# A wavelet convolution: two more images loaded ahead of the second half, and a shorter hand-over of the first batch's last coefficients

## The chip, the cores and the metric

The kernel runs on one core of one Trainium2 chip. The metric is the device time of one execution in microseconds (us), lower is better. The time of a kernel is the median over its runs.

## The reference

The input `x` has 8 batches of 32 channels, each channel a 512x512 float32 image (1 MB). Each image goes through a four-level wavelet transform. The coarsest level (a low band and three detail bands of 42x42 each, 84x84 together) is mixed over the channels, for each coefficient with a 32x32 matrix of its own; the finer detail bands stay as they are. Then the transform is inverted.

```
yl, yh = _dwt2(x, 4)
yl_out = einsum('bixy,ioxy->boxy', yl, w_yl)
yh_out = yh[:-1] + [einsum('bicxy,iocxy->bocxy', yh[-1], w_yh)]
return _idwt2(yl_out, yh_out)
```

Since all steps are linear and the finer bands come back unchanged, the output is `x` plus the inverse transform of (mixed minus unmixed coarse coefficients). That is how the kernel computes it.

## The kernel before

It works in three phases, with an order written out by hand for each engine and semaphores between them.

Phase 1 (from the start to about 662 us) reads all 256 images once, on SP's queue, and reduces each to 84x84 coefficients.

The mixing (to about 739 us) goes through 32 pieces (`PIECES`), of the 84x84 coefficients of all batches. SP loads the weights of a piece into a ring of four places in `work` (`w_sb`, `load_w`). ScalarE and VectorE spread the coefficients of a piece into a diagonal operand (`diag`, two of them, `build_high` and `build_low`), TensorE multiplies (`mix`, L474 and L479), ScalarE copies the sums from PSUM into `mix_sb` (`copy_mixed`, L611). Along with it, the coefficients of the first batch to be written (batch 7) are brought into the form that phase 2 needs, in six steps v = 0 to 5: ScalarE copies a step from `mix_sb` to `first_stage` (`copy_first`, L618), TensorE turns it (`first_coefs`, L488), ScalarE copies it to `delta` (`copy_delta`, L627). The last step, v = 5 (`FULL`), needs the sums of the last piece, number 31.

Phase 2 (to the end) reads the images again, adds the correction and writes them, batch 7 first. The image of one channel takes: a copy of its coefficients to `pick` (`pick_image`, L667, ScalarE), a matrix product (`spread_stage`, L518), a copy (`copy_spread`, L673), four products (`out_stage`, L528), two additions on VectorE (`add`, L759), in place in the buffer of the image, and the store (`store`, L344, on SP's queue). One turn is eight images (`SLOTS`), for the eight buffers of `x_sb`; there are 32 turns. The eight images of turn 0 are still in `x_sb` from phase 1. GpSimd (POOL) refills a buffer when its store has landed (`refill`, L280), in the order of its own instructions: what stands first in it holds up all behind it.

Of the images of turn 1, number 8 to 15 of phase 2, the first six (`EARLY` = 6) are loaded ahead into `work`, which is no longer needed by then (`load_early`, L320 and L323): three during phase 1 and the mixing, and three behind the last pieces. They are stored from there (L351). Images 14 and 15 come by a refill of buffers 6 and 7 of `x_sb`. So the refills are: images 16 to 21 for buffers 0 to 5 and 14 and 15 for buffers 6 and 7 behind the stores of turn 0; then images 22 and 23 for buffers 6 and 7, behind the stores of images 14 and 15; then turn by turn.

The other things that lie in `work`: `w_sb` at 6784 to 13952 (in elements of a partition), `diag` at 13952 to 17536, and in phase 2 `delta` for two batches in turn, 2688 elements each from 4096 and from 13000, and `stage` (the next batch's coefficients, L658) from 15688. The early images lie at 0, 2048, 19184, 6784, 8832 and 10880, 2048 elements each.

Of the kernel before, what the change touches and what calls it, by code (L numbers as in the profile page):

```python
# [22 lines left out]
BATCH, CHANNELS, SIZE = 8, 32, 512  # L23
# [29 lines left out]
TURNED = {1: 0, 2: 1, 4: 2, 5: 3, 7: 4, 8: 5}  # L53
IDLE = ROUNDS + 1 - STEPS

EARLY = 6

WARM = 9

# [83 lines left out]
def last_piece(s):  # L143
    return len(LEFT) + PARTS * s - 1


def wavelet_mix_kernel(nc, x, w_full, w_left, consts, out):
# [3 lines left out]
    with ExitStack() as ctx:  # L151
# [41 lines left out]

        early = [0, IMAGE, AT_EARLY] + [AT_W + IMAGE * e for e in range(EARLY - 3)]
        early = [work[:, e:e + IMAGE].rearrange("p (r w) -> p r w", r=ROW_RUN) for e in early]
        APART = -(-(AT_W + IMAGE * (EARLY - 3) - 2 * IMAGE) // ROWS)
        at = 2 * IMAGE + (APART + CHANNELS) * ROWS
        delta = work[:, 2 * IMAGE:at].rearrange("p (a r) -> p a r", r=ROWS)
        assert at + STEPS * Q * ROWS <= AT_EARLY
# [69 lines left out]
        @block.gpsimd  # L269
        def _(pool):  # L270
            nc.gpsimd.memset(work[:, IMAGE:AT_W], 0.0).then_inc(pass1_cleared, 1)
            nc.gpsimd.memset(mix_sb[:, 0], 0.0).then_inc(cleared, 1)
            nc.gpsimd.memset(pick[:], 0.0).then_inc(cleared, 1)
            nc.gpsimd.memset(spread[:], 0.0).then_inc(cleared, 1)


            def refill(c, t, first):

                pool.wait_ge(x_stored[c], 16 * (t - (c < EARLY)))
                pool.dma_start(x_sb[:, c], x_rows[first + c]).then_inc(x_reloaded[c], 16)  # L280

            for c in range(SLOTS):
                if c < EARLY:
                    refill(c, 2, IMAGES - 3 * SLOTS)
                else:
                    refill(c, 1, IMAGES - 2 * SLOTS)
            for c in range(EARLY, SLOTS):
                refill(c, 2, IMAGES - 3 * SLOTS)
            with pool.Fori(3, TURNS) as t:
                first = t * -SLOTS + (IMAGES - SLOTS)  # L290
                for c in range(SLOTS):
                    refill(c, t, first)

        @block.sync
        def _(sp):
            sp.dma_start(const[:, 0:SW], consts[:, 0:SW]).then_inc(const_loaded, 16)


            for c in range(SLOTS):
                sp.dma_start(x_sb[:, c], x_rows[c]).then_inc(x_loaded[c], 16)  # L300
                if c == GROUP - 1:
                    sp.dma_start(const[:, SW:CONSTS], consts[:, SW:CONSTS]).then_inc(more_loaded, 16)
            with sp.Fori(1, TURNS) as t:
                for c in range(SLOTS):
                    if c % GROUP == 0:
                        sp.wait_ge(h_done[c // GROUP], t)
                    sp.dma_start(x_sb[:, c], x_rows[SLOTS * t + c]).then_inc(x_loaded[c], 16)  # L307


            def load_w(k):  # L310
                c = k % RING
                if k < len(LEFT):
                    u = LEFT[k]
                    sp.dma_start(w_sb[:, c, 0:u * 4 * CHANNELS], w_left[k, :, 0:u * 4 * CHANNELS]).then_inc(w_loaded[c], 16)
                else:
                    sp.dma_start(w_sb[:, c], w_full[k - len(LEFT)]).then_inc(w_loaded[c], 16)

            def piece_mixed(k):

                sp.wait_ge(mixed[k % 2], k // 2 + 1)  # L320

            def load_early(e):
                sp.dma_start(early[e], x_rows[IMAGES - 2 * SLOTS + e]).then_inc(early_loaded[e], 16)  # L323

            for k in range(RING):
                load_w(k)
            load_early(2)
            sp.wait_ge(t_done, TURNS * SLOTS)
            load_early(0)
            sp.wait_ge(c_done, TURNS * HALVES + 1)  # L330
            load_early(1)
            for k in range(RING, PIECES):
                piece_mixed(k - RING)
                load_w(k)
            for e in range(3, EARLY):
                piece_mixed(PIECES - RING + e - 3)
                piece_mixed(PIECES - RING + e - 2)
                load_early(e)

            def store(c, t, first):
                sp.wait_ge(added[1], SLOTS * t + c + 2)
                sp.dma_start(out_rows[first + c], x_sb[:, c]).then_inc(x_stored[c], 16)  # L344

            for c in range(SLOTS):
                store(c, 0, IMAGES - SLOTS)
            for c in range(SLOTS):
                if c < EARLY:
                    sp.wait_ge(added[1], SLOTS + c + 2)  # L350
                    sp.dma_start(out_rows[IMAGES - 2 * SLOTS + c], early[c]).then_inc(early_stored, 16)  # L351
                else:
                    store(c, 1, IMAGES - 2 * SLOTS)
            with sp.Fori(2, TURNS) as t:
                first = t * -SLOTS + (IMAGES - SLOTS)
                for c in range(SLOTS):
                    store(c, t, first)
            sp.wait_ge(early_stored, 16 * EARLY)
            for c in range(SLOTS):
                sp.wait_ge(x_stored[c], 16 * (TURNS - (c < EARLY)))  # L360

        @block.tensor
        def _(pe):
# [149 lines left out]
            def spread_stage(c, t):  # L513

                p, n = c % 2, SLOTS // 2 * t + c // 2
                pe.wait_ge(picked[p], n + 1)
                pe.wait_ge(s_copied[p], n + 1)
                nc.tensor.matmul(ps[0:ROWS, p], pick[:, p], const[:, SW:SW + SIZE],  # L518
                                 start=True, stop=True).then_inc(s_done[p], 1)

            def out_stage(c, t):

                p, n = c % 2, SLOTS * t + c
                pe.wait_ge(s_copied[p], SLOTS // 2 * t + c // 2 + 2)
                for half in range(2):
                    pe.wait_ge(added[half], n + 1)
                    for k in (2 * half, 2 * half + 1):
                        last = nc.tensor.matmul(ps[:, 2 + k], const[:, SH + P * k:SH + P * k + P], spread[:, p],  # L528
                                                start=True, stop=True)
                    last.then_inc(o_done[half], 1)  # L530
# [10 lines left out]
                        coefs_stage(2 * (c - 1) + 1, batch)  # L541

            pe.wait_ge(cleared, 4)
            spread_stage(0, 0)
            with pe.Fori(0, BATCH - 1) as k:
                with pe.Fori(0, TURNS_BATCH - 1) as r:
                    turn2(TURNS_BATCH * k + r)
# [6 lines left out]
        def _(act):  # L554
# [59 lines left out]
            def copy_first(v, i):  # L614
# [3 lines left out]
                nc.scalar.copy(first_stage[:].rearrange("p (q r) -> p q r", q=Q), mix_sb[:, v, :, :, BATCH - 1],  # L618
                               ).then_inc(first_staged, 1)

            def copy_delta(v, k, done):
                n, h = lines(v), first_row(v)
                bank = (6 + v % 2) if done is None else 6
                act.wait_ge(d_done, STEPS * k + v + 1 + IDLE if done is None else done)
                to = delta[0:ROWS, bass.ds(APART * (k & 1), CHANNELS), h:h + Q * n]
                of = ps[0:ROWS, bank].rearrange("p (q l o) -> p o l q", q=Q, l=4)[:, :, 0:n]
                nc.scalar.copy(to.rearrange("p o (l q) -> p o l q", q=Q), of).then_inc(d_copied, 1)  # L627
# [9 lines left out]
            for k in range(PIECES):  # L637
                if k % RING == 0 and k // RING not in TURNED:
                    act.sem_inc(first_staged, 1)
                if k + 2 < PIECES:  # L640
                    build_high(k + 2)
                copy_mixed(k)
                i, j = divmod(k, RING)
                if j == 2:
                    if i in TURNED:
                        copy_delta(TURNED[i], 0, i + 1)
                    else:
                        act.wait_ge(d_done, i + 1)
                        act.sem_inc(d_copied, 1)
                for at, v in TURNED.items():  # L650
                    if k == last_piece(v):
                        copy_first(v, at)


# [19 lines left out]

            def turn2(t, last=False, batch=None):
                for c in range(SLOTS):
                    if batch is not None and 2 <= c <= 4:
                        copy_delta(2 * (c - 2), batch, None)
                        copy_delta(2 * (c - 2) + 1, batch, None)
# [13 lines left out]

            copy_delta(FULL, 0, ROUNDS + 1)
            act.wait_ge(d_copied, STEPS + IDLE + 1)
            pick_image(0, 0)
            pick_image(1, 0)
            copy_spread(0, 0)
            with act.Fori(0, BATCH - 1) as k:
# [8 lines left out]
        def _(dve):  # L708
# [53 lines left out]
            for c in range(SLOTS):  # L762
                add(c, 0, x_sb[:, c])
            for c in range(SLOTS):
                if c < EARLY:
                    dve.wait_ge(early_loaded[c], 16)
                    add(c, 1, early[c])
                else:
                    dve.wait_ge(x_reloaded[c], 16)
                    add(c, 1, x_sb[:, c])  # L770
            with dve.Fori(2, TURNS) as t:
                for c in range(SLOTS):
                    dve.wait_ge(x_reloaded[c], 16 * (t - (c < EARLY)))
                    add(c, t, x_sb[:, c])


# [25 lines left out]
```

## Time and profile before

| | |
|---|---|
| median of 3 runs | 1996.33 us (1993.37 to 1996.72) |
| the profiled execution | 2000.08 us, its span 1998.4 us |
| mean granted clock of TensorE | 0.994 |
| busy: PE, DVE, ACT, POOL | 94%, 41%, 24%, 7% |
| moved by DMA | 827.04 MB, 414 GB/s over the span |
| read, written | 558.29 MB, 268.44 MB |

The engines in the rows are PE (TensorE matmul), PEld (its weight load), DVE (VectorE), ACT (ScalarE), POOL (GpSimd), SP (SyncE, which only issues transfers here). Times of the trace are us from the start of the span. The span lies 1.7 us below the profiled execution's time. A matrix product in float32 appears as two MATMUL records.

### The profile page before, as it was taken

Reading aid. Unit: us, or ns where it says so; the run is one execution under the profiler, and the core shown is the slowest. Engines: PE = TensorE matmul, PEld = TensorE weight load, DVE = VectorE, ACT = ScalarE, POOL = GpSimd, SP = SyncE. Lnnn points to the kernel's source line nnn. Section 1 sums busy time; section 2 is a strip of 40 time slices with the busy share of each in tenths; the row PEclk is TensorE's granted clock in tenths of the full one; section 3 lists DMA queues with packets and bytes.
Section 4 is the critical chain, followed back from the end, with each engine's and each line's share of the span. In section 5 each row is a group of like instructions: output and inputs, shape, how many; then the busy total and the mean of one; then the engine's idle time right before and its main releaser. Section 6 shows DMA issues by size and latency. Waiting matters only on the chain.

```text
span 1998.4 us, 44611 instructions
## 1 busy us (share of the span) xinstructions
PE 1873.2 (94%) x17701; PEld 939.1 (47%) x17701; DVE 810.9 (41%) x931; ACT 483.7 (24%) x1055; POOL 135.7 (7%) x250
## 2 busy tenths in 40 slices
PE   8999999999999899999999999999999999999996
PEld 5666666666666554444343343343343343333332
DVE  2222222222222345555444444444444444444443
ACT  2233232332332551221221121121121121122110
POOL 1000000000000000011111111111111111111110
PEclk9999999999999999999999999999999999999999
DMA  9999999999999899999999999999999999999997
GB/s 369 415 415 421 418 422 422 422 422 422 422 422 421 313 375 387 367 427 427 427 427 427 427 427 427 427 427 427 427 427 427 427 427 426 416 427 419 417 425 336
DMA packets 114355, 827.04 MB, mean 414 GB/s; under 512 B 12704, under 2 KB 12704, under 8 KB 17056
## 3 DMA queue, kind: packets, MB, share of 16 engines
q1 hardware_dynamic: 79488, 573.01, 68.9%
q0 software_dynamic: 34848, 253.77, 30.4%
q8 instruction: 13, 0.21, 0.0%
q14 instruction: 6, 0.05, 0.0%
HBM read 558.29 MB, written 268.44 MB: 414 GB/s over the span
## 4 chain that ended last, share of the span: by engine, by line
DMA 61%; PE 30%; issue 4%; DVE 2%; SPq 1%; ACT 0%; DVEq 0%; POOLq 0%; ACTq 0%
DMA out<-x_sb 33%; DMA x_sb<-x 28%; PE ps L388 10%; PE ps L528 7%; PE ps L401 5%; DVE x_sb L759 2%; PE ps L518 2%; PE ps L479 2%; PE ps L474 2%; SPq L307 1%; PE ps L412 1%; PE ps L420 1%; PE ps L434 1%; ACT mix_sb L581 0%; PE ps L488 0%
## 5 line engine op out<-in xcount | busy, mean ns | idle before, releaser
L528 PE MATMUL ps<-spread,const 128*128 128x512 f32 x2048 | 940.1, 602 | 75.4 <-DVE x_sb L759 75.4
L759 DVE TENSOR_TENSOR x_sb<-ps,x_sb 128x1024 f32<-128x1024 f32 x500 | 592.9, 1221 | 632.2 <-DMA x_sb<-x 546.9
L528 PEld LDWEIGHTS ps<-spread,const 128*128 128x128 f32 x2048 | 373.5, 190 | 640.0 <-issue 406.8
L673 ACT COPY spread<-ps 84x512 f32<-84x512 f32 x256 | 148.8, 581 | 923.9 <-PE ps L518 922.4
L388 PE MATMUL ps<-x_sb,const 32*32 32x512 f32 x8192 | 286.7, 597 | 20.6 <-DMA x_sb<-x 17.3
L401 PEld LDWEIGHTS ps<-const,work 128*128 128x128 f32 x2048 | 246.6, 193 | 52.6 <-ACT work L565 38.1
L518 PE MATMUL ps<-const,pick 128*84 128x512 f32 x512 | 261.3, 592 | 1.0 <-issue 1.0
L401 PE MATMUL ps<-const,work 128*128 128x84 f32 x2048 | 255.6, 277 | 0.0
L280 POOL DMA_DIRECT2D x_sb<-x x242 | 128.1, 529 | 1837.0 <-DMA out<-x_sb 1837.0
L565 ACT COPY work<-ps 128x512 f32<-128x512 f32 x256 | 131.4, 600 | 416.6 <-PE ps L388 416.6
L388 PEld LDWEIGHTS ps<-x_sb,const 32*32 32x32 f32 x8192 | 138.1, 103 | 119.7 <-issue 79.7
L718 DVE COPY work<-ps 128x336 f32<-128x336 f32 x256 | 130.0, 508 | 153.3 <-PE ps L401 153.3
L724 DVE COPY work<-ps 128x336 f32<-128x336 f32 x65 | 33.0, 508 | 338.0 <-PE ps L412 338.0
L518 PEld LDWEIGHTS ps<-const,pick 128*84 128x84 f32 x512 | 77.3, 153 | 121.9 <-issue 121.9
L667 ACT COPY pick<-work 84x84 f32 (+1 forms) x256 | 66.7, 261 | 10.7 <-issue 10.7
L744 DVE COPY work<-mix_sb 32x448 f32<-32x448 f32 (+1 forms) x96 | 36.4, 379 | 39.5 <-PE ps L479 36.3
L412 PE MATMUL ps<-work,const 128*32 128x336 f32 x520 | 50.8, 463 | 0.6 <-DVE work L718 0.6
L420 PE MATMUL ps<-work,const 128*84 128x336 f32 x130 | 48.2, 452 | 0.6 <-DVE work L724 0.6
L479 PEld LDWEIGHTS ps<-work 128*32 128x32 f32 x3584 | 37.3, 110 | 21.6 <-DMA work<-w_full 10.7
L479 PE MATMUL ps<-work 128*32 128x32 f32 x3584 | 38.1, 199 | 3.3 <-issue 3.3
L627 ACT COPY work<-ps 84x512 f32 (+3 forms) x48 | 24.0, 529 | 55.8 <-PE ps L508 54.4
L571 ACT COPY work<-ps 84x336 f32 (+1 forms) x65 | 28.2, 434 | 37.6 <-PE ps L420 37.6
(30 smaller groups left out, 301.4 us busy)
## 6 DMA issues: line engine op xcount, KB each, us to landing
x_sb<-x SPq DMA_DIRECT2D x256, 1024.0 KB, 10.1
out<-x_sb SPq DMA_DIRECT2D x250, 1024.0 KB, 24.6
x_sb<-x POOLq DMA_DIRECT2D x242, 1024.0 KB, 11.7
work<-w_full SPq DMA_DIRECT2D x30, 896.0 KB, 7.3
work<-x SPq DMA_DIRECT2D x6, 1024.0 KB, 5.6
out<-work SPq DMA_DIRECT2D x6, 1024.0 KB, 9.7
work<-w_left SPq DMA_DIRECT2D x1, 896.0 KB, 15.0
const<-consts SPq DMA_DIRECT2D x1, 592.0 KB, 12.2
```

The costliest lines, as they stand in the source:

```text
L280: pool.dma_start(x_sb[:, c], x_rows[first + c]).then_inc(x_reloaded[c], 16)
L388: last = nc.tensor.matmul(ps[to:to + TILE, m], const[part, A3H + TILE * r:A3H + TILE * r + TILE], x_sb[part, GROUP * a + m, r], start=r == ...
L401: last = nc.tensor.matmul(ps[:, 4 + m % 2, ROWS * k:ROWS * k + ROWS], along_h[:, m, P * k:P * k + P], const[:, A4 + ROWS * m:A4 + ROWS * ( ...
L412: last = nc.tensor.matmul(ps[TILE * k:TILE * k + TILE, 6, 0:GROUP * ROWS], const[:, at:at + TILE], turned[:, k].rearrange("p m r -> p (m r ...
L420: nc.tensor.matmul(ps[0:ROWS, 7, 0:GROUP * ROWS], const[:, A4:A4 + ROWS], third, start=True, stop=True).then_inc(c_done, 1)
L479: last = nc.tensor.matmul(ps[32 * l:32 * l + 32, j, QB * u:QB * u + QB], w[:, u, l], diag[:, a, l, u], start=False, stop=u == U - 1)
L518: nc.tensor.matmul(ps[0:ROWS, p], pick[:, p], const[:, SW:SW + SIZE], start=True, stop=True).then_inc(s_done[p], 1)
L528: last = nc.tensor.matmul(ps[:, 2 + k], const[:, SH + P * k:SH + P * k + P], spread[:, p], start=True, stop=True)
L565: nc.scalar.copy(along_h[:, m], ps[:, m]).then_inc(h_copied, 1)
L673: nc.scalar.copy(spread[0:ROWS, p], ps[0:ROWS, p]).then_inc(s_copied[p], 1)
L718: nc.vector.tensor_copy(turned[:, :, m], ps[:, 4 + m % 2, 0:SEGS * ROWS].rearrange("p (k r) -> p k r", k=SEGS),).then_inc(t_copied, 1)
L759: nc.vector.tensor_tensor(part, ps[:, 2 + 2 * half:4 + 2 * half], part, ALU.add).then_inc(added[half], 1)
```

## The change

The program loads eight early images. `EARLY` is 8; the two new ones lie at 12928 and 14976, over the last place of the weight ring and both diagonal operands, so that they are loaded, like image 5 of the early ones, behind the matmuls of piece 31. All of turn 1 is then computed in `work` and stored from there, and POOL's first eight refills are for turn 2. The second `delta` and `stage` move down and overlap early images 5 to 7, so ScalarE waits for all early stores at the start of turn 3, ahead of the first copies of the next batch.

The last step of the first batch is split. The 70 of 84 columns that come from pieces 26 to 30 are copied from `mix_sb` behind `copy_mixed(30)` (`copy_last_first`), and the 14 columns of piece 31 are copied from PSUM straight to `first_stage` ahead of `copy_mixed(31)` (`copy_last_piece`). The first image's product reads its coefficients from `delta` and not from `pick` (`first_spread`).

```diff
-EARLY = 6
+EARLY = 8
...
-        APART = -(-(AT_W + IMAGE * (EARLY - 3) - 2 * IMAGE) // ROWS)
+        APART = -(-(AT_W + IMAGE * 2 - 2 * IMAGE) // ROWS)
...
             def refill(c, t, first):
-                pool.wait_ge(x_stored[c], 16 * (t - (c < EARLY)))
+                pool.wait_ge(x_stored[c], 16 * (t - 1))
                 pool.dma_start(x_sb[:, c], x_rows[first + c]).then_inc(x_reloaded[c], 16)
             for c in range(SLOTS):
-                if c < EARLY:
-                    refill(c, 2, IMAGES - 3 * SLOTS)
-                else:
-                    refill(c, 1, IMAGES - 2 * SLOTS)
-            for c in range(EARLY, SLOTS):
                 refill(c, 2, IMAGES - 3 * SLOTS)
...
             for e in range(3, EARLY):
-                piece_mixed(PIECES - RING + e - 3)
-                piece_mixed(PIECES - RING + e - 2)
+                piece_mixed(min(PIECES - RING + e, PIECES + 1) - 3)
+                piece_mixed(min(PIECES - RING + e, PIECES + 1) - 2)
                 load_early(e)
...
             for c in range(SLOTS):
-                if c < EARLY:
-                    sp.wait_ge(added[1], SLOTS + c + 2)
-                    sp.dma_start(out_rows[IMAGES - 2 * SLOTS + c], early[c]).then_inc(early_stored, 16)
-                else:
-                    store(c, 1, IMAGES - 2 * SLOTS)
+                sp.wait_ge(added[1], SLOTS + c + 2)
+                sp.dma_start(out_rows[IMAGES - 2 * SLOTS + c], early[c]).then_inc(early_stored, 16)
...
+            def first_spread():
+                pe.wait_ge(d_copied, STEPS + IDLE + 1)
+                nc.tensor.matmul(ps[0:ROWS, 0], delta[0:ROWS, CHANNELS - SLOTS], const[0:ROWS, SW:SW + SIZE],
+                                 start=True, stop=True).then_inc(s_done[0], 1)
...
-            spread_stage(0, 0)
+            first_spread()
...
+            def copy_last_first():
+                n = U * (PARTS - 1)
+                act.wait_ge(mixed_copied, RING + PIECES - 1)
+                act.wait_ge(d_done, ROUNDS)
+                nc.scalar.copy(first_stage[:].rearrange("p (q r) -> p q r", q=Q)[:, :, 0:n],
+                               mix_sb[:, FULL, :, 0:n, BATCH - 1])
+            def copy_last_piece():
+                k, n = PIECES - 1, U * (PARTS - 1)
+                act.wait_ge(mixed[k % 2], k // 2 + 1)
+                (_, of), = sums_of(k)
+                nc.scalar.copy(first_stage[:].rearrange("p (q r) -> p q r", q=Q)[:, :, n:ROWS],
+                               of[:, :, :, BATCH - 1]).then_inc(first_staged, 1)
...
+                if k == PIECES - 1:
+                    copy_last_piece()
                 copy_mixed(k)
+                if k == PIECES - 2:
+                    copy_last_first()
...
-                    if k == last_piece(v):
+                    if k == last_piece(v) and v < FULL:
                         copy_first(v, at)
...
+                    if batch is not None and c == 0:
+                        act.wait_ge(early_stored, 16 * EARLY)
...
-            pick_image(0, 0)
+            act.sem_inc(picked[0], 1)
             pick_image(1, 0)
...
             for c in range(SLOTS):
-                if c < EARLY:
-                    dve.wait_ge(early_loaded[c], 16)
-                    add(c, 1, early[c])
-                else:
-                    dve.wait_ge(x_reloaded[c], 16)
-                    add(c, 1, x_sb[:, c])
+                dve.wait_ge(early_loaded[c], 16)
+                add(c, 1, early[c])
```

## Rows read from the trace of the kernel before

**Rows 1.** The page, the span in 40 slices of 50 us: share of DMA, rate.
```profile
DMA  9999999999999899999999999999999999999997
GB/s 369 415 415 421 418 422 422 422 422 422 422 422 421 313 375 387 367 427 427 427 427 427 427 427 427 427 427 427 427 427 427 427 427 426 416 427 419 417 425 336
```

**Rows 2.** The page, the chain that ended last, by engine.
```profile
DMA 61%; PE 30%; issue 4%; DVE 2%; SPq 1%; ACT 0%; DVEq 0%; POOLq 0%; ACTq 0%
```

**Rows 3.** Chain in order of time: start, us, what; one image and the last transfers.
```profile
808.85 3.43 PE ps L528 x8
812.28 0.86 PE ps L518 x2
...
1947.42 24.67 DMA out<-x_sb
...
1972.84 11.67 DMA x_sb<-x
```

**Rows 4.** Stretches: length, busy time of each engine, PEclk, DMA share, GB/s.
```profile
740.00:744.60 4.60, 2.83 (x9) 1.20 (x10) 0.00 (x0) 2.48 (x7) 0.00 (x0) 1.00 0.99 388
744.60:750.50 5.90, 5.90 (x15) 2.57 (x14) 2.45 (x2) 1.45 (x5) 0.00 (x0) 1.00 0.12 47
...
806.00:815.00 9.00, 9.00 (x22) 3.84 (x21) 5.00 (x5) 1.58 (x4) 0.53 (x1) 1.00 0.63 259
```

**Rows 5.** Timeline of SP's queue, 730 to 860 us: start, time from first to last.
```profile
735.03 4.69 SPq L323 DMA_DIRECT2D work<-x  x3
749.20 30.38 SPq L344 DMA_DIRECT2D out<-x_sb  x8
783.53 21.79 SPq L351 DMA_DIRECT2D out<-work  x6
809.28 47.69 SPq L344 DMA_DIRECT2D out<-x_sb  x12
```

**Rows 6.** Timeline of POOL: the 1st, 8th, 9th, 16th, 42nd, 201st, 209th and last refill.
```profile
753.76 0.66 POOL L280 DMA_DIRECT2D x_sb<-x  x1 [745.49 <-DMA out<-x_sb]
...
789.51 0.54 POOL L280 DMA_DIRECT2D x_sb<-x  x1 [4.53 <-DMA out<-x_sb]
813.54 0.53 POOL L280 DMA_DIRECT2D x_sb<-x  x1 [23.49 <-DMA out<-x_sb]
...
850.75 0.53 POOL L280 DMA_DIRECT2D x_sb<-x  x1 [4.34 <-DMA out<-x_sb]
...
978.42 0.53 POOL L280 DMA_DIRECT2D x_sb<-x  x1 [4.38 <-DMA out<-x_sb]
...
1768.87 0.53 POOL L280 DMA_DIRECT2D x_sb<-x  x1 [4.42 <-DMA out<-x_sb]
...
1808.97 0.53 POOL L280 DMA_DIRECT2D x_sb<-x  x1 [4.58 <-DMA out<-x_sb]
...
1972.84 0.54 POOL L280 DMA_DIRECT2D x_sb<-x  x1 [4.45 <-DMA out<-x_sb]
```

**Rows 7.** Timeline at the end of the mixing, ACT and PE, and one copy in turn 2.
```profile
737.81 0.58 ACT L627 COPY work<-ps 84x512 f32<-84x512 f32 x1
...
739.35 0.53 ACT L611 COPY mix_sb<-ps 128x448 f32<-128x448 f32 x1 [0.96 <-PE ps L479]
739.91 0.79 ACT L618 COPY const<-mix_sb 128x336 f32<-128x336 f32 x1
...
740.76 0.64 PE L488 MATMUL ps<-const 128*84 128x128 f32 x4 [1.45 <-ACT const L618]
741.43 0.58 ACT L627 COPY work<-ps 84x512 f32<-84x512 f32 x1 [0.73 <-PE ps L488]
742.04 0.42 ACT L667 COPY pick<-work 84x84 f32<-84x84 f32 x2
...
742.40 1.92 PE L518 MATMUL ps<-const,pick 128*84 128x512 f32 x4 [1.01 <-issue]
...
843.30 0.58 ACT L673 COPY spread<-ps 84x512 f32<-84x512 f32 x1 [3.55 <-PE ps L518]
```

More of the change, by code:

```diff
@@ L359, in _ @@
             for c in range(SLOTS):
-                sp.wait_ge(x_stored[c], 16 * (TURNS - (c < EARLY)))
+                sp.wait_ge(x_stored[c], 16 * (TURNS - 1))
         @block.tensor
@@ L764, in _ @@
             for c in range(SLOTS):
-                if c < EARLY:
-                    dve.wait_ge(early_loaded[c], 16)
-                    add(c, 1, early[c])
-                else:
-                    dve.wait_ge(x_reloaded[c], 16)
-                    add(c, 1, x_sb[:, c])
+                dve.wait_ge(early_loaded[c], 16)
+                add(c, 1, early[c])
             with dve.Fori(2, TURNS) as t:
                 for c in range(SLOTS):
-                    dve.wait_ge(x_reloaded[c], 16 * (t - (c < EARLY)))
+                    dve.wait_ge(x_reloaded[c], 16 * (t - 1))
                     add(c, t, x_sb[:, c])
```

## The prediction

> **What bounds the kernel now.** I read the slices of the page first: the DMA engines are busy in nearly all of them, at up to 427 GB/s, and the low slices (313, 375, 387, 367 GB/s) all lie between 650 and 850 us, where the phases change [rows 1]. The chain says the same: 61% of the span is DMA and 30% PE [rows 2]. So what counts is where the DMA engines stand idle, and the view to go to is the one of stretches. Loads end at about 744.6 us; in the 5.9 us behind that the DMA share is 0.12, since the mixing is over and no image has been finished; and from 806 to 815 it is 0.63 [rows 4].
>
> The second gap shows in the queues. SP stores one image after the other: 8 from `x_sb` from 749.20 on, 6 from `work`, and the next at 809.28, which is 14 images on, so (809.28 - 749.20) / 14 = 4.29 us for an image [rows 5]. That is PE's own time, 0.86 for the spread product and 3.43 for the four others [rows 3]. This stretch goes at PE's pace. POOL issues its first 8 refills from 753.76 to 789.51 us, and then nothing for 23.5 us: its ninth needs the store of image 14 and comes at 813.54 [rows 6]. Meanwhile the DMA engines have one store of 1.05 MB per 4.29 us, 2.46 us of work at 427 GB/s, a share of 0.57, as seen.
>
> From the ninth refill on it is otherwise. From refill 42 at 978.42 to refill 242 at 1972.84 there are 200, at 4.97 us each [rows 6]: a load and a store, 2.10 MB, at 422 GB/s. For a while PE still runs ahead on images loaded early, but that uses up a lead and doesn't move the end. At the end the chain is store, refill, addition, store [rows 3]. So I cut the time in two at the ninth refill: ahead of it the pace is PE's, behind it the DMA engines'.
>
> **The hand-over, part by part.** In the profile the last piece's sums are ready at 739.35. Then follow in one line the copy to `mix_sb` (0.53), the copy to `first_stage` (0.79), the turning on PE (from 740.76, 0.64), the copy to `delta` (from 741.43, 0.58), the pick (from 742.04, two in 0.42), and the first product at 742.40: 3.05 us [rows 7]. With the change the copy of 14 columns comes first. No row shows it: 128 partitions x 56 elements. Its ends are 0.21 us (half of the 0.42 for two copies of 84 columns) and 0.53 (a copy of 448 from PSUM) [rows 7]; I take 0.26, near the small one. Then 739.35 + 0.26 + 0.06 (from copy to PE) + 0.67 (PE start to the next copy's start) + 0.58 + 0.10 = 741.0. The copy to `mix_sb` moves behind it and ends at about 740.1, under PE's turning. Gain 1.4 us, with the large copy 1.1.
>
> The 70-column copy is new on ACT behind `copy_mixed(30)`, ahead of the copy of step 4 to `delta`. ACT has 739.35 - 738.39 = 0.96 us free there [rows 7]; it takes about 0.79 x 280 / 336 = 0.66, at most 0.79. It is covered with 0.2 to 0.3 us to spare; if copies in a row that depend on each other add a little, the gain falls to 0.9. I keep 0.9 to 1.4. Its waits are on work that ended before.
>
> **The two early images.** Their loads go to SP's queue behind piece 31, right behind the load of image 5 of the early ones [rows 5]. They take 2 x 2.46 = 4.9 us, from 744.6 to 749.5, nearly all of the first gap [rows 4]. The first store, issued 1.4 us earlier at 747.8, stands behind them in the queue and lands at about 752.9, not 753.8; that costs nothing, as refills 1 to 8 (now images 16 to 23) are far ahead of their use. Nothing waits for the two images until 744 + 14 x 4.29 = 804 us.
>
> What it moves is the cut. POOL's ninth refill is now image 24, which needs the store of image 16. PE's pace holds until there: that store is issued at 749.20 - 1.4 + 16 x 4.29 = 816.5 and lands after 813.54 - 809.28 = 4.26 us, at 820.7 [rows 5, 6]. That is 7.2 us later than before, as the idle gap at 806 grows by two more images. Behind it, there are 240 refills in all and not 242, so the last comes 231 and not 233 periods later: 2 x 4.97 = 9.9 us less. The lead of the loads on PE at the cut is the same as before (refill 9 with images 15 to 17 in work there), so what follows should repeat itself two images later.
>
> **The added wait.** ScalarE waits at turn 3 for all early stores. Behind it are queued its picks and spread copies, and PE behind them. It gets there at about 843.9 - 1.4 us, by its last copy of turn 2 at 843.30 [rows 7]; the last early store, of image 15, is issued at 812.1 and lands some 4 to 6 us later. More than 20 us of slack: nothing. The other edits (smaller semaphore counts, one product from `delta`) cost nothing that a row could show; the PE clock is at 1.00 in both stretches of the hand-over [rows 4].
>
> **Sum.** -1.4 (hand-over) + 2 x 4.29 - 2 x 4.97 = -2.76 us. In other words: two more images go at PE's pace and not at DMA's, which returns 0.68 us each, not the 4.9 us that their loads take. The profiled execution of 2000.08 us would become 1997.3. It stands 3.75 us above the median; taken off the median, 1996.33 - 2.76 = 1993.6 us, a gain of 0.14%. About 0.2%, 4.0 us, is what a measurement of this kernel can tell from no change, so the likeliest verdict is no difference.
>
> **A rule against the row.** The 4.97 us per image is 422 GB/s with one core at work [rows 6]. The Trainium skill (DMA: Bandwidth & Descriptors, section Where 436 GB/s comes from) says that for transfers between HBM and SBUF the HBM side binds, at about 358 GB/s. By that an image would cost 5.86 us and the sum would be -1.4 - 2 x (5.86 - 4.29) = -4.5 us, an estimate from that page; the trace disagrees with it in every slice of phase 2, and the sum goes by the trace.
>
> **The rivals.**
> 1. A larger gain, by the restart. Behind the ninth refill the transfers find their order anew: refills 9 to 16 take 850.75 - 813.54 = 37.2 us for 7 periods, 2.4 us more than 7 x 4.97; refills 1 to 8 took 35.75, 1.0 more [rows 6]. If the restart is better when it begins in order at buffer 0, up to 2.4 us come on top: 1991.2. If the bytes alone counted, as a DMA share of 61% in the chain suggests [rows 2], the two loads would return all of their 4.9 us and with the hand-over 6.3: 1990.0. Against that speaks the gap at 806, which grows. Together 0.27.
> 2. A memory-bound pace as in the restart (5.32 us per image there): -1.4 - 2 x (5.32 - 4.29) = -3.5 us, 1992.9, still within 0.2%. The later rows hold it for 200 refills at 4.97. 0.02.
> 3. Slower, by the pace of the loop of 8 buffers. The steady pace isn't given by the bytes alone: turns differ, and the one from 1768.87 to 1808.97 has 5.01 per refill [rows 6]. The new start may lock loads and stores into another pattern. Over 231 periods 0.012 us more in each (4.984) eats the gain, and 0.029 (5.001) makes it slower by 0.2%. At 5.01 throughout it would be 231 x 0.04 = 9.3 us, with the gain 2002.8; with half of that 1998.2. One turn of 25 is like that, so 0.07.
> 4. It doesn't do what it says: the 70-column copy isn't covered, and the restart loses 1 to 2 us more than before, since image 16's store has to share with image 17's. 1995 to 1996.5; 0.06.
>
> **How the numbers follow.** Forecast 0.58, rivals 0.27, 0.02, 0.07, 0.06. Rival 1 is faster by over 0.2% in most cases, and the forecast's own spread (0.9 to 1.4 for the hand-over, about 1.5 for the restart) passes the bound now and then: faster 0.27, within 0.2% 0.66, slower 0.07. The range reaches from rival 1's far half to rival 4's upper end: 1990.2 to 1996.8 leaves out about half of rival 1's lowest case and rival 3.
>
> **What would show it.** Right: the first L518 at about 741.0; the last early loads landing at 749 to 750 with no gap in DMA ahead of the first store; no refill of POOL from about 789 to 821, with a DMA share near 0.57 from 806 to 820; the ninth refill at 820.7 and the last, number 240, near 1970; 4.97 us between late refills. Wrong: another steady pace, a ninth refill well before 820, ScalarE waiting at turn 3, or a restart that takes more or less than 37 us for its first 7 periods.

## The result and the profile after

The changed kernel takes 1993.61 us in the median of 12 runs (1991.11 to 1995.31), the kernel before in the same series 1997.30 us (12 runs, 1993.37 to 2001.31). The ratio is 0.9977, with a 95% interval of 0.9968 to 0.9986: 4.6 us less by the ratio, 3.7 by the medians. Forecast were 2.76 us less. Two more measurements on other chips, told below, gave 0.9985 and 0.9983.

The profiled execution of the changed kernel has a span of 1991.8 us, 6.6 us below that of before. I take it apart along the path that the prediction laid out.

The timeline at the end of the mixing, ACT and PE; it answers to [rows 7]:

```profile
735.08 0.72 ACT L625 COPY const<-mix_sb 128x280 f32<-128x280 f32 x1
...
736.49 0.21 ACT L633 COPY const<-ps 128x56 f32<-128x56 f32 x1 [0.20 <-PE ps L472]
736.59 0.54 ACT L610 COPY mix_sb<-ps 128x448 f32<-128x448 f32 x1
...
736.75 0.64 PE L481 MATMUL ps<-const 128*84 128x128 f32 x4 [0.30 <-ACT const L633]
737.42 0.58 ACT L642 COPY work<-ps 84x512 f32<-84x512 f32 x1 [0.29 <-PE ps L481]
...
738.14 1.06 PE L517 MATMUL ps<-const,work 84*84 84x512 f32 x2 [0.76 <-ACT work L642]
```

The last sums are ready at 736.49 and the first product of phase 2 starts at 738.14: 1.65 us, where it was 3.05. The copy of 14 columns (L633) has 0.21 us, that of 70 columns (L625) 0.72, and the latter is over before it could be in the way: ACT waits 0.20 us for PE ahead of L633. But the sums themselves are ready 2.86 us earlier than in the profile of before. The first load behind the mixing goes out the same 2.86 us earlier, and what the change puts ahead of the last sums is only the copy of 70 columns, which is work more and not less; so this part doesn't come from the change.

SP's queue, then POOL's refills: the 1st, 8th, 9th, 16th and last. They answer to [rows 5] and [rows 6].

```profile
732.17 5.64 SPq L319 DMA_DIRECT2D work<-x  x5
744.93 30.38 SPq L340 DMA_DIRECT2D out<-x_sb  x8
779.27 30.37 SPq L346 DMA_DIRECT2D out<-work  x8
813.77 44.09 SPq L340 DMA_DIRECT2D out<-x_sb  x11
```

```profile
751.38 0.66 POOL L281 DMA_DIRECT2D x_sb<-x  x1 [743.11 <-DMA out<-x_sb]
...
786.74 0.54 POOL L281 DMA_DIRECT2D x_sb<-x  x1 [3.95 <-DMA out<-x_sb]
818.44 0.53 POOL L281 DMA_DIRECT2D x_sb<-x  x1 [31.16 <-DMA out<-x_sb]
...
856.13 0.53 POOL L281 DMA_DIRECT2D x_sb<-x  x1 [4.41 <-DMA out<-x_sb]
...
1966.00 0.53 POOL L281 DMA_DIRECT2D x_sb<-x  x1 [4.43 <-DMA out<-x_sb]
```

Five early loads go out from 732.17, the first store follows 12.76 us behind the first of them (14.17 before). From the first store to the ninth refill it is 73.51 us (64.34 before), from there to the last refill 1147.56 (1159.30 before), from there to the end 25.8 (25.6 before). So the 6.6 us are: 2.9 ahead of the sums, 1.4 in the hand-over, -9.2 up to the ninth refill, 11.7 behind it, -0.2 at the end. Of the 11.7, two periods of 4.97 are 9.9; the other 1.8 are 231 periods that were each 0.008 us shorter.

The stretches of [rows 4] in the changed kernel:

```profile
740.00:744.60 4.60, 4.60 (x12) 2.07 (x12) 2.14 (x2) 0.90 (x3) 0.00 (x0) 1.00 1.00 399
744.60:750.50 5.90, 5.90 (x15) 2.54 (x14) 2.76 (x3) 1.48 (x4) 0.00 (x0) 1.00 0.87 368
806.00:815.00 9.00, 9.00 (x22) 3.84 (x21) 4.97 (x5) 1.49 (x5) 0.00 (x0) 1.00 0.58 239
...
804.00:820.00 16.00, 16.00 (x39) 6.93 (x38) 9.12 (x8) 3.07 (x8) 0.53 (x1) 1.00 0.57 235
```

The first gap is gone (a DMA share of 0.87 where it was 0.12), and the second is longer: 16 us at a share of 0.57. Since all marks lie 2.86 us earlier here, the stretch that stands as far behind the last sums as 744.6 to 750.5 did before is 741.7 to 747.6: there the share is 1.00 at 418 GB/s. That is the exchange: the two loads fill the first gap, and the second takes most of the gain back.

### The profile page after: what moved, and what is told of

It reads as the page before. It is cut to its first block, busy times and chain, and to the rows that moved or that the text cites. A ratio compares the mean times of both kernels' runs of the same rounds, so it can differ in the third digit from the quotient of the medians.

```text
span 1991.8 us, 44554 instructions
## 1 busy us (share of the span) xinstructions
PE 1870.6 (94%) x17701; PEld 936.8 (47%) x17701; DVE 810.4 (41%) x931; ACT 483.7 (24%) x1055; POOL 134.7 (7%) x248
## 4 chain that ended last, share of the span: by engine, by line
DMA 61%; PE 30%; issue 4%; DVE 2%; SPq 1%; ACT 0%; DVEq 0%; POOLq 0%; ACTq 0%
DMA out<-x_sb 32%; DMA x_sb<-x 29%; PE ps L381 10%; PE ps L527 7%; PE ps L394 5%; DVE x_sb L780 2%; PE ps L511 2%; PE ps L472 2%; PE ps L467 1%; SPq L303 1%; PE ps L405 1%; PE ps L413 1%; PE ps L427 1%; ACT mix_sb L580 0%; PE ps L481 0%
## 5 line engine op out<-in xcount | busy, mean ns | idle before, releaser
L527 PE MATMUL ps<-spread,const 128*128 128x512 f32 x2048 | 940.2, 602 | 73.5 <-DVE x_sb L780 73.5
L765 DVE COPY work<-mix_sb 32x448 f32<-32x448 f32 (+1 forms) x96 | 36.4, 379 | 37.5 <-PE ps L472 32.4
L472 PE MATMUL ps<-work 128*32 128x32 f32 x3584 | 37.5, 198 | 3.5 <-issue 3.5
```

The lines of the kernel that those rows point to most:

```text
L472: last = nc.tensor.matmul(ps[32 * l:32 * l + 32, j, QB * u:QB * u + QB], w[:, u, l], diag[:, a, l, u], start=False, stop=u == U - 1)
```

## The experiments

The theory: up to the ninth refill the time goes at PE's pace, behind it at the DMA engines'; the change gives 1.4 us by the hand-over and about 1.4 by two images that change sides. Its rivals: the bytes alone count; the restart behind the ninth refill gives more; the gain is chance.

**The hand-over alone.** On the kernel before:

```diff
-            spread_stage(0, 0)
+            first_spread()
...
+                if k == PIECES - 1:
+                    copy_last_piece()
                 copy_mixed(k)
+                if k == PIECES - 2:
+                    copy_last_first()
```

> The kernel before with the hand-over alone (the 14 columns straight from PSUM, the first product from delta); six early images. Two-pace theory: the first product comes 1.4 us earlier behind the last piece's sums, PE's pace carries that to the ninth refill, and the end comes 1.4 us earlier (ratio to before 0.9993). Rival, bytes alone: the loads and stores that are left are the same, so 0. Rival, a chance difference of the profiled executions ahead of the mixing: a change of 1 to 3 us that is not there in this one.

Measured: 1995.22 us (12 runs), ratio 0.9990 with 0.9980 to 1.0000. Its first product (737.66) comes as soon behind the last sums as in the changed kernel, and the first store 12.9 us behind the first of the early loads from `x`. From the first store to the ninth refill it has 64.32 us, as before. The place of the gain in the trace is as the theory has it; its size, 2.0 us by the ratio, can't be told from 1.4, and hardly from 0.

**The early images alone.** The changed kernel with the hand-over of before:

```diff
-EARLY = 6
+EARLY = 8
...
             spread_stage(0, 0)
```

> The changed kernel with the hand-over of before; eight early images. Two-pace theory: two images at 4.29 us and not at 4.97, 1.4 us less (ratio to before 0.9993); the ninth refill stands 8.6 us later behind the first store than before, at 64.3 + 8.6 = 72.9 us. Rival, bytes alone: both loads come back whole, 4.9 us less (0.9975), and the measured 3.7 to 4.6 us of the whole change would be nearly all from here. Rival, restart: 1.4 us and up to 2.4 more.

Measured: 1995.93 us, ratio 0.9989 with 0.9979 to 0.9999. From the first store to the ninth refill 73.50 us, the same as in the changed kernel. The 4.9 us (0.9975) of the bytes alone lie outside the interval, if only just. The traces say it more clearly. From the first store to the end the five profiles of kernels with eight early images and nothing else changed behind the first store (the changed kernel three times, this run, and the later start below) have 1245.3 to 1247.7 us, in the mean 1246.9; the three with six (the kernel before twice, and the hand-over alone) have 1246.6 to 1249.2, in the mean 1247.5. That is 0.6 us less and not 4.9: the rival that the loads come back whole is out. That each half holds a part of the gain is what the traces show; by the totals alone it isn't shown, since the changed kernel's ratios lie inside the intervals of both halves.

**The changed kernel again.** No edit.

> The changed kernel once more, on the same chip as its two halves. Two-pace theory: the sum of the halves, 2.8 us less than before (0.9986). Measured earlier: 0.9977 with an interval of 0.9968 to 0.9986; if it comes near 0.9977 again, 1.9 us are not explained by the sum. The granted clock at 662 us and the pace of the late refills are to be compared in this profile: before had 0.50 there and 4.97 us, the changed kernel 1.00 and 4.96.

Measured: 1994.03 us, ratio 0.9985 with 0.9974 to 0.9996. From the first store to the ninth refill 73.52 us; from the ninth to the 16th refill 37.1 us (37.7 in its first profile, 37.2 before). The restart is the same, so rival 1's first reason is out too.

**The gap filled.** Places 0 to 4 of the early images are free for all of phase 2 once they are stored. Five images of turn 3 are loaded there, right behind the first eight refills:

```diff
+            for c in range(AGAIN):
+                pool.wait_ge(early_stored[c], 16)
+                pool.dma_start(early[c], x_rows[IMAGES - 4 * SLOTS + c]).then_inc(early_again[c], 16)
+            for c in range(AGAIN):
+                refill(c, 4, IMAGES - 5 * SLOTS)
             for c in range(AGAIN, SLOTS):
                 refill(c, 3, IMAGES - 4 * SLOTS)
```

`AGAIN` is 5, `early_stored` is a semaphore for each place, and SP and VectorE take these five images from `work`.

> The changed kernel with five images of turn 3 loaded into the places in work that are free from then on, behind the stores of the early images there. Two-pace theory: the idle time of DMA between the eighth and the ninth refill (804 to 820 us at a share of 0.57, 6.9 us idle) is filled with 5 loads of 2.46 us, and the restart behind it falls away (up to 2.4 us): 5 to 9 us less than the changed kernel, ratio to before 0.993 to 0.9955. Rival, the gap is idle time that costs nothing because the steady loop of eight buffers sets the end: no gain over the changed kernel, 0.9977.

Measured: 1987.95 us (5 runs), ratio 0.9949 with 0.9936 to 0.9962. On another chip, next to the changed kernel:

> The kernel with the gap filled, on the same chip as the changed kernel. Two-pace theory: as measured, 6 to 7 us less than the changed kernel, ratio to before 0.9949 again.

Measured: 1986.54 us (6 runs), ratio 0.9938 with 0.9924 to 0.9952; the changed kernel there 1994.38. It is 6 to 8 us faster than the changed kernel and 10 to 12 faster than the one before. POOL's refills in this second profile, the 8th to the 10th and the 13th and 14th, and its stretches:

```profile
785.27 0.54 POOL L288 DMA_DIRECT2D x_sb<-x  x1 [3.46 <-DMA out<-x_sb]
790.11 0.53 POOL L291 DMA_DIRECT2D work<-x  x1 [4.31 <-DMA out<-work]
795.08 0.53 POOL L291 DMA_DIRECT2D work<-x  x1 [4.43 <-DMA out<-work]
...
809.74 0.53 POOL L291 DMA_DIRECT2D work<-x  x1 [4.32 <-DMA out<-work]
825.57 0.53 POOL L284 DMA_DIRECT2D x_sb<-x  x1 [15.30 <-DMA out<-x_sb]
```

```profile
804.00:820.00 16.00, 16.00 (x38) 6.81 (x37) 9.05 (x8) 3.07 (x8) 1.06 (x2) 1.00 1.01 427
820.00:840.00 20.00, 20.00 (x48) 8.53 (x47) 11.75 (x10) 3.76 (x10) 2.12 (x4) 1.00 1.01 426
...
860.00:900.00 40.00, 40.00 (x101) 17.50 (x100) 22.60 (x19) 8.00 (x21) 2.65 (x5) 1.00 0.95 375
```

The refills run on through 809.74, and from 804 to 820 the DMA engines are at 1.01 and 427 GB/s. The 6.9 us that stood idle there in the changed kernel are about what the end gains. POOL still pauses 15.3 us, but loads are queued up then. From 860 to 900 a small gap is left (0.95). That the idle time of DMA in this place is worth its length at the end is shown, within the some 3 us that the intervals leave, and that it costs nothing is out.

**A later start.** Ten more products of 128x512 behind the last turning, on the changed kernel:

```diff
             first_coefs(ROUNDS)
+            for n in range(10):
+                nc.tensor.matmul(ps[:, 7], const[:, 0:P], const[:, 0:SIZE], start=True, stop=True)
```

> The changed kernel with ten more 128x512 products on TensorE behind the last turning of the hand-over (10 x 0.86 = 8.6 us, of which 0.75 fall into PE's wait for the copy to delta), so the first product of phase 2 comes 7.9 us later behind the last sums. Two-pace theory: a late start of phase 2 costs its whole length at the end, +7.9 us over the changed kernel, and 1.4 us of hand-over are 1.4 us of the end. Rival, the lead of the loads or the early images cover part of the start: less than +4.

Measured: 2001.27 us (10 runs), ratio 1.0018 with 1.0006 to 1.0031. From the first early load to the first store 20.39 us, 7.63 more than in the changed kernel. Against the changed kernel's three ratios (mean 0.9982) the time is 0.0036 up, 7.2 us. Behind the first store nothing gave way: 73.50 us to the ninth refill and 1247.1 to the end, as in the changed kernel. A late start costs its whole length. That the hand-over's 1.4 us are 1.4 at the end is concluded from this; the totals can't resolve it.

**More work for PE, ahead of the cut and behind it.** One more product of 256 columns in an image, `extra` set in turns 0 and 1, or in three turns of four from turn 4 to 27:

```diff
                     out_stage(c, t)
+                    if extra:
+                        nc.tensor.matmul(ps[:, 7, 0:256], const[:, 0:P], const[:, 0:256], start=True, stop=True)
```

> The changed kernel with one more product of 256 columns on TensorE for each of the 16 images of turns 0 and 1 (0.43 us each by half of 0.86; the spacing of the stores will tell). Two-pace theory: this stretch goes at PE's pace, so the ninth refill comes 16 x 0.43 = 6.9 us later and the end with it. Rival, the whole of phase 2 is bound by DMA: 0.

> The changed kernel with the same added product for each of the 144 images of three turns in four from turn 4 to 27: 62 us of added PE work. Two-pace theory: behind the ninth refill the pace is DMA's, 4.96 against 4.29 + 0.43 = 4.72, so 0 to +1 us. Rival, PE sets the pace in part, or the steady pace of 4.96 depends on how long an image takes between its load and its store (one of three stations of the loop of eight buffers): +144 x a part of 0.43, up to 60 us.

Measured: ahead of the cut 2003.30 us, ratio 1.0021 (1.0007 to 1.0036), which is 7.8 us over the changed kernel's 0.9982. SP's queue and the ninth refill of this kernel:

```profile
746.22 33.40 SPq L340 DMA_DIRECT2D out<-x_sb  x8
784.00 33.40 SPq L346 DMA_DIRECT2D out<-work  x8
821.96 4.60 SPq L340 DMA_DIRECT2D out<-x_sb  x2
```

```profile
826.64 0.53 POOL L281 DMA_DIRECT2D x_sb<-x  x1 [37.36 <-DMA out<-x_sb]
```

The stores come every 4.72 us, and the ninth refill 80.42 us behind the first store, 6.9 later, as expected. Behind the cut: 1996.15 us, ratio 0.9988 (0.9973 to 1.0004), 1.2 us over 0.9982, which lies inside the interval of 3 us to each side, for 62 us of added work. PE's waits for the additions fell from 73.5 us to 22.6: the added work went mostly into time in which PE stood idle. Its refills from the ninth on come every 4.98 us. These two runs show the cut most plainly: 6.9 us of PE work cost 7.8 on one side of it, 62 us cost about nothing on the other.

**Thirteen buffers.** The five places in `work` stay in use to the end, for every second turn:

```diff
+            with pool.Fori(2, TURNS // 2) as j:
+                for c in range(AGAIN):
+                    load_x(c, 2 * j, j)
+                for c in range(AGAIN, SLOTS):
+                    load_x(c, 2 * j - 1, 2 * j - 2)
+                for c in range(AGAIN):
+                    load_e(c, 2 * j + 1, j)
+                for c in range(AGAIN, SLOTS):
+                    load_x(c, 2 * j, 2 * j - 1)
```

> The kernel with the gap filled, and the five places in work kept in use to the end: 13 buffers and not 8, buffers 0 to 4 of x_sb in even turns, the five in work in odd ones. It asks what sets the steady pace. If the loop of eight buffers holds it at 4.95 to 4.97 us for an image (before, refills 9 to 41 went at 4.91 while PE ran ahead): with five more buffers 4.91, so 200 x 0.05 = 8 to 12 us less than the kernel with the gap filled, about 1977 us. Rival, 4.95 is what the DMA engines give for loads and stores in turn, whatever the buffers: no change, 1986 to 1988 us.

> The kernel with thirteen buffers, on the same chip as the one with the gap filled. If the count of buffers sets the steady pace, it is 8 to 12 us faster than that one; if the DMA engines set it, the same within 2 us. Its first profile had 1241.2 us from the first store to the end against 1237.7 with the gap filled, which speaks for the second.

Measured: 1985.24 us (4 runs, 0.9928, 0.9908 to 0.9948) and on the other chip 1986.83 (6 runs, 0.9940, 0.9925 to 0.9956), next to 1986.54 with the gap filled. On one chip the two are 0.3 us apart, and the 8 to 12 us are not there. The totals alone would not settle it, since this kernel has an idle stretch of its own near the end: from 1900 to 1950 us its DMA share is 0.90 and 0.89 in its two profiles, where it is 1.01 with the gap filled. The pace does settle it: from the 60th to the 200th refill one takes 4.97 us in both profiles with thirteen buffers, 4.95 and 4.96 with the gap filled, and the DMA share from 1000 to 1400 us is 1.01 in all of them, so that the lower clock told of below doesn't hide a gain either. So more buffers don't make the steady pace faster.

The 4.91 us that the expectation names held for refills 16 to 42 in the first profile of before (from the ninth on it is 5.00, with the restart). The three profiles of the changed kernel show such a step too, from 4.91 to 4.92 us before it to 4.96 to 4.97 behind it. The second profile of before, told of next, doesn't: there these refills took 4.97 each, and those from the 60th to the 200th 4.95. Why the pace went from 4.91 us to 4.97 near 973 us stays open.

**What two equal kernels differ by.**

> The kernel before, once more, with a second profile. It gives what two equal kernels differ by here: ratio 1.000 and an interval of about 0.001 to each side. In its profile the first store to the ninth refill should be 64.3 us again (PE's pace), while the granted clock at 662 us and the pace of the late refills (4.97 before, 4.95 to 4.97 elsewhere) are free to differ: if they do, they belong to the execution and not to the change.

> The changed kernel a third time. By the parts as the traces measured them (hand-over -1.4, two early images +9.2 - 9.9 = -0.8) -2.2 us, ratio 0.9989; by the prediction's sum 0.9986; by the first two measurements 0.9977 and 0.9985. A third ratio near 0.998 would leave about 1.5 us that no part of the sum holds.

Measured: the kernel before 1996.45 us, ratio 0.9994 (0.9982 to 1.0006); the changed kernel 1994.38, ratio 0.9983 (0.9973 to 0.9994). The second profile of the kernel before has a span of 1994.7 us. Its store of image 14 and its ninth and last refills:

```profile
748.08 30.38 SPq L344 DMA_DIRECT2D out<-x_sb  x8
782.41 21.79 SPq L351 DMA_DIRECT2D out<-work  x6
808.16 47.68 SPq L344 DMA_DIRECT2D out<-x_sb  x12
```

```profile
813.37 0.53 POOL L280 DMA_DIRECT2D x_sb<-x  x1 [22.81 <-DMA out<-x_sb]
...
1970.08 0.54 POOL L280 DMA_DIRECT2D x_sb<-x  x1 [4.39 <-DMA out<-x_sb]
```

From the first store to the ninth refill it has 65.29 us, not the 64.3 expected: the store of image 14 took 5.2 us to land and not 4.3. From there 233 periods take 1156.7 us, 4.964 each, against 4.976 in the first profile. The early loads start at 733.91, not 735.03. So an equal kernel was 3.7 us shorter in its span: 1.1 by its start, 2.6 by the pace and 0.9 behind the last refill, less 0.95 for the landing of that store.

## Why the prediction was right

**The range and the direction held.** Forecast 1993.6 us, measured 1993.61. That the two agree so closely is luck: the forecast was 2.76 us off a median of 1996.33, and with more runs the kernel before lies at 1997.3 to 1998.5 by the series. In the first series the start was 1.0 us too low and the gain 0.9 too small, and the two cancel. What was forecast is the difference: 2.76 us, against 4.6, 3.0 and 3.4 us by the three ratios (0.9977, 0.9985, 0.9983), in the mean 3.7. The first is past the 0.2% below which no difference was forecast, the others are short of it; the mean of 0.18% stands at that bound.

**The hand-over** was sized right to the last step: 1.65 us from the sums to the first product, as worked out (739.35 to 741.0), a gain of 1.40. The copy without a row took 0.21 us, the small end; the 70 columns took 0.72 in the expected 0.66 to 0.79 and were covered. The run with a later start shows that a delay in this place reaches the end whole.

**The two images** were right in kind. The ninth refill came 73.51, 73.52 and 73.50 us behind the first store in the profiles of the changed kernel, where 72.9 were forecast. Of the difference of 0.6 us, 0.4 is landing: 4.67 us for the store of image 16, where 4.26 was taken from one store; the other 0.2 is that 16 images took 68.84 us and not 68.64. In the kernel before the landing is not fixed either (64.34 and 65.29 us from the first store to the ninth refill). So this term is 9.9 - 9.2 to 9.9 - 8.2, 0.8 to 1.7 us, with the forecast 1.36 in it. With the hand-over the traces hold 2.2 to 3.1 us of the 3.7. With the 2.86 us by which the first profile of the changed kernel runs early added, the ninth refill lies at 821.3 (forecast 820.7) and the last at 1968.9 (near 1970). Its first store landed 6.45 us behind its issue, not 5.1, and as worked out this cost nothing.

**The rest**, some 1 us, is not explained. The interval of each ratio is about 2 us to each side, that of the mean of the three by the same figures about 1.2 (an estimate), so it may be nothing; I have no mechanism for it.

**The rivals.** The bytes alone: out, since eight early images alone gained 2.2 us and not 4.9, since the time from the first store to the end fell by 0.6 us and not by 4.9, and since the second gap grew to 16 us as worked out. A better restart: out, 37.7, 37.1 and 37.4 us for refills 9 to 16 against 37.2 and 37.5. A pace of 5.32 us behind the cut (rival 2): out, by the mean periods that follow. That it doesn't do what it says (rival 4): out, since the copy of 70 columns was covered and the restart took no longer. The pace of the loop: it does differ, and by about the amount priced, but between executions of one kernel. The mean period behind the ninth refill was 4.976 and 4.964 us in the two profiles of before, 4.968, 4.961 and 4.969 in the changed kernel, 4.964 to 4.980 in the single changes. 0.011 us, by which the two profiles of before differ, are 2.6 us over 231 periods, nearly the whole change. In the mean it is 4.968 us in the three profiles with six early images and the same in the five with eight: no sign that the change moved it.

**The added wait** on ScalarE cost nothing that shows: in the first profile of the changed kernel the copies of the next batch start at 843.81, right behind the last copy of turn 2 (843.33), with no idle time of ScalarE between them.

**The rule of the Trainium skill** that HBM binds at about 358 GB/s (DMA: Bandwidth & Descriptors, Where 436 GB/s comes from) has no support here: with the gap filled, one core moves 427 GB/s from 804 to 820 us. By it the change would have given 4.5 us; the first measured ratio alone could not have told, but the rates in the rows do. The prediction says that the trace of before disagrees in every slice of phase 2; the last slice, which ends with idle time, has 336 GB/s and is the exception.

The prediction said of the second gap that it grows, and used that only to lower the gain. Filling it gives 6 to 8 us, more than the whole change: the row of [rows 4] with a share of 0.63 was the larger find.

## What to carry to other kernels

Where a phase goes at one engine's pace first and at DMA's later, find the event at which it changes over (here a refill that waits for a store) and count on each side of it: work moved across gains only the difference of the two paces, not its own length. Idle time of DMA ahead of such a change-over is worth its length at the end only if filling it opens no new gap. Here the two loads in the first gap made the second one longer and returned 0.8 to 1.7 us of their 4.9; five loads in the second gap, into places that were already free, returned about its whole length. So look for such buffers at the last gap ahead of the change-over. And when a change is worth less than the scatter of executions (here 3 to 4 us of 2000), compare marks within the traces, from one event to the next, since most of them repeat to a few hundredths of a microsecond where the totals don't (73.50 to 73.52 us up to the ninth refill in the changed kernel). Not all do: in the kernel before the same stretch was 64.34 and 65.29 us.

## What the runs showed of the hardware that was not expected

The time ahead of the last sums and the pace of the transfers vary more from one execution to the next than the change is worth: the first load behind the mixing was issued anywhere from 730.0 to 735.4 us in the fourteen profiles of these kernels, whose code is the same up to the last two pieces, and the mean period behind the ninth refill lay between 4.961 and 4.980 us in the ten profiles of kernels without the gap filled.

TensorE's granted clock at the end of phase 1 was one of the things that varied. Three stretches of the first profile of before, and of the second:

```profile
660.00:662.00 2.00, 1.20 (x5) 0.63 (x6) 0.22 (x1) 0.43 (x1) 0.00 (x0) 0.91 0.94 397
662.00:664.00 2.00, 2.00 (x16) 2.00 (x16) 1.44 (x5) 1.87 (x5) 0.00 (x0) 0.50 1.01 340
664.00:666.00 2.00, 2.00 (x14) 0.92 (x16) 0.52 (x2) 2.00 (x5) 0.00 (x0) 0.50 0.60 254
```

```profile
660.00:662.00 2.00, 1.30 (x10) 0.38 (x10) 0.53 (x2) 0.00 (x0) 0.00 (x0) 1.00 0.63 209
662.00:664.00 2.00, 1.48 (x17) 1.21 (x17) 0.38 (x2) 1.22 (x4) 0.00 (x0) 1.00 1.05 365
664.00:666.00 2.00, 1.63 (x53) 0.98 (x54) 1.57 (x5) 1.98 (x5) 0.00 (x0) 1.00 0.93 393
```

In the first the granted clock is at half, 1.2 GHz, from 662 us; in the second, of the same code, it stays at 2.4. PE did the same ahead of it in both: three waits of 0.60, 0.63 and 0.53 us for VectorE and ScalarE at the end of phase 1, the last of them over at 661.59 in the first and at 662.80 in the second. Why the clock fell in one only stays open. Of the changed kernel's three profiles one had the half clock there, of all fourteen profiles four. With thirteen buffers it fell again and again in phase 2, first here:

```profile
970.00:980.00 10.00, 6.18 (x15) 2.39 (x14) 3.08 (x4) 1.56 (x4) 1.05 (x2) 1.00 1.01 428
980.00:985.00 5.00, 5.00 (x9) 2.04 (x8) 1.86 (x3) 0.00 (x0) 0.53 (x1) 0.66 1.01 428
```

PE was busy 6.18 us of 10 there (it waited 3.8 us at once for an addition), and in the next 5 us the granted clock was 0.66. That kernel's mean clock was 0.98, and on the same chip its time was within 0.3 us of the one with the gap filled, whose mean clock was 1.00.
